# AdaLN modulation in a two-layer transformer kernel: shift and scale made as columns by one-column products

## Chip, core and metric

The kernel runs as one program on one core of a Trainium2 chip. The metric is the device time of a run in microseconds (us), from its first to its last instruction; the median of three runs is compared. Names of engines in the rows: PE is TensorE (matmul), PEld its weight loads, DVE is VectorE, ACT is ScalarE, POOL is GpSimd, SP is SyncE, which issues DMAs.

## What is computed

Two transformer layers over x (1024 rows of 512). Each has an attention branch and a feed-forward branch, and before each branch the rows are layernormed, scaled and shifted by vectors that come from a condition c (AdaLN); a third vector gates the branch's output. From the reference:

```python
mod = (_silu(L0_c) @ L0_wmod).reshape(L0_c.shape[0], 6, 1, -1)
sa, ca, ga, sb, cb, gb = (mod[:, 0], mod[:, 1], mod[:, 2], mod[:, 3], mod[:, 4], mod[:, 5])
ga = (2 * (ga >= 0) - 1) * jnp.maximum(jnp.abs(ga), 0.25)
gb = (2 * (gb >= 0) - 1) * jnp.maximum(jnp.abs(gb), 0.25)
h = _layernorm(x, axis=-1) * (1 + ca) + sa
x = x + ga * _L0_attn_ref(h, ...)
h = _layernorm(x, axis=-1) * (1 + cb) + sb
x = x + gb * _L0_ffn_ref(h, ...)
# the same again for layer 1, with L1_c, L1_wmod and its own attention and experts
```

Here c is 1 x 512 and wmod 512 x 3072, both f32, so each of the six vectors of a layer is a product of one row of 512 with a 512 x 512 matrix. The branches are a quantized attention, a low-rank-adapted feed-forward, a second attention, and a mixture of experts with low-rank adapters.

## The kernel before

The program is a row of phases; each is a block in which every engine has its own instruction stream, and no engine enters a block before all have left the last. Within a block, semaphores order the engines. The edit touches the four layernorm phases (`layernorm_phase`, run 0 to 3, called here first, second, third and fourth stage: 0 to 44 us, 979 to 1015.5, 1236.6 to 1263.5 and 1728.8 to 1752.6) and the output phase of the second attention (`layer1_output_phase`, 1681 to 1700 us).

`Modulation` holds the 512 x 512 f32 parts of wmod as SBUF tiles, 128 partitions by 4 blocks k by 512 (`mod0a_w`, `mod0b_w`, `mod1a_w`, `mod1b_w`). `silu_c` holds silu(c) as columns, 128 partitions by layer and k. `make_silu_rows` (L146) has VectorE copy each column broadcast to a 128 x 128 tile `silu_rows` (four tiles), with which as stationary operand a matmul yields the same row of 512 on all 128 partitions. Such a row is what a gate needs (`make_row` L181, `take_gate` L186), since a gate multiplies along the free axis.

Scale and shift are needed per partition instead, since the layernormed rows are first transposed (L313, so that a feature is a partition) and ScalarE applies them as its per-partition `scale` and `bias` (L335, L338). `make_columns` (L159) therefore makes the two rows in PSUM banks 4 and 5, by 8 matmuls of 512 moving columns, each f32 in two passes, and `take_columns` (L166) reads the diagonal: VectorE multiplies each 128 x 128 block of the row with the identity and sums it (L173, eight times, four columns for shift and four for scale, into `column`), and adds one to the scale (L178). `column_made`, `diagonals` and `column_taken` are the semaphores of these steps, `rows_done` that of `silu_rows`.

A layernorm phase on each engine:

- VectorE: `silu_rows`, then for each half of the rows (four tiles of 128 x 512) statistics (L254, L257), variance plus epsilon (L261), ScalarE's square root awaited, a reciprocal (L265) with one Newton step, and the normalised tiles (L276). In the second half it takes the columns: behind the normalised tiles in stages one to three, before the reciprocal in the fourth (`gate_first`). In the fourth stage it next takes the gate (L192 to L197). Then come eight pieces of `hT`, high and low parts for the split products of the next phase: ScalarE writes the high part of even pieces, VectorE casts that of odd ones (L286) and subtracts all low parts (L288), at last the gate in stage two.
- TensorE: first of all the columns' product, then (fourth stage only) the gate's row, then eight pieces of four transposes each (L313), at last the gate's row in the first and second stage. The third stage has no gate; that of its layer is made in the output phase, after two pieces.
- ScalarE: loads of weights in some stages, the two square roots (L326), then, when `column_taken` says so, the affine steps L335 and L338 in the order of the pieces, with four buffers.
- GpSimd works in the second stage on the weights of the feed-forward (L1084 among others). SyncE issues the loads of wmod.

In the output phase TensorE transposes `attended` (L1894) piece by piece, ScalarE copies each out (L1920), VectorE subtracts; VectorE makes `silu_rows` ahead of that.

## Time and profile before

| | us |
|---|---|
| Median of the three runs | 1811.9 |
| Lowest and highest of them | 1811.73, 1813.33 |
| The profiled execution | 1815.9 |
| Span in its trace | 1814.0 |
| TensorE busy | 1675.2 (92%) |
| TensorE's weight loads | 1344.5 (74%) |
| VectorE busy | 1192.8 (66%) |
| ScalarE busy | 1008.7 (56%) |
| GpSimd busy | 724.9 (40%) |

All times of rows are us from the start of the span. The profiled execution is one execution of the program, 4.0 us above the median of the timed ones; shares of busy time are averages over all phases, so that a stage of 30 us has to be read by its own rows.

### The profile page before, as it was taken

Reading aid. Unit: us, or ns where it says so; the run is one execution under the profiler, and the core shown is the slowest. Engines: PE = TensorE matmul, PEld = TensorE weight load, DVE = VectorE, ACT = ScalarE, POOL = GpSimd, SP = SyncE. Lnnn points to the kernel's source line nnn. Section 1 sums busy time; section 2 is a strip of 40 time slices with the busy share of each in tenths; the row PEclk is TensorE's granted clock in tenths of the full one; section 3 lists DMA queues with packets and bytes.
Section 4 is the critical chain, followed back from the end, with each engine's and each line's share of the span. In section 5 each row is a group of like instructions: output and inputs, shape, how many; then the busy total and the mean of one; then the engine's idle time right before and its main releaser. Section 6 shows DMA issues by size and latency. Waiting matters only on the chain. (4 is left out here: it accounts for less than half of the span.)

```text
span 1814.0 us, 28444 instructions
## 1 busy us (share of the span) xinstructions
PE 1675.2 (92%) x10115; PEld 1344.5 (74%) x10115; DVE 1192.8 (66%) x2924; ACT 1008.7 (56%) x2229; POOL 724.9 (40%) x656
## 2 busy tenths in 40 slices
PE   4899999999999999999997799996779999999778
PEld 2698999999999999899885588784645555554557
DVE  5667777677677777777667533355876777773475
ACT  2477777777877777777773211102216666666131
POOL 3286675756747567485531200000532222211200
PEclk8999999999999999999999899997959999999889
DMA  7101000000010100100003112005000000000021
GB/s 187 37 13 30 19 24 26 23 30 18 25 36 13 30 19 24 30 13 24 18 7 88 67 53 65 2 1 184 1 1 1 1 1 1 1 1 1 30 45 47
DMA packets 72358, 56.07 MB, mean 31 GB/s; under 512 B 23023, under 2 KB 54447, under 8 KB 72219
## 3 DMA queue, kind: packets, MB, share of 16 engines
q1 hardware_dynamic: 70634, 53.47, 10.2%
q8 instruction: 83, 1.36, 0.3%
q10 hardware_dynamic: 1584, 0.79, 0.2%
q14 instruction: 57, 0.46, 0.1%
HBM read 52.14 MB, written 2.10 MB: 30 GB/s over the span
## 5 line engine op out<-in xcount | busy, mean ns | idle before, releaser
L746 PEld LDWEIGHTS psum<-a_probsT,a_v 128*128 128x128 f32 x2304 | 294.7, 191 | 25.6 <-issue 3.9
L746 PE MATMUL psum<-a_probsT,a_v 128*128 128x128 f32 x2304 | 299.2, 275 | 1.7 <-ACT a_probsT L956 1.6
L845 DVE CUSTOM_DVE_ANT_0 psum<-psum,a_keys_allowed 128x128 f32<-128x128 f32 (+7 forms) x256 | 195.7, 764 | 83.0 <-PE psum L77 74.4
L939 ACT ACTIVATE a_probs<-psum,a_neg_max 128x128 f32<-128x128 f32 (+7 forms) x256 | 190.7, 745 | 66.6 <-DVE a_neg_max L845 58.2
L1827 ACT ACTIVATE a_probsT<-psum 128x512 f32<-128x512 f32 (+3 forms) x384 | 174.6, 497 | 86.4 <-PE psum L1664 62.4
L948 ACT ACTIVATE a_probs<-a_probs,a_row_inv 128x128 f32<-128x128 f32 (+7 forms) x256 | 201.1, 786 | 27.9 <-DVE a_row_inv L852 27.7
L609 POOL TENSOR_TENSOR a_turned_pool<-a_q_sum,a_sine 64x512 f32<-64x512 f32 x62 | 79.3, 1278 | 287.8 <-DVE a_q_sum L831 286.6
L875 DVE TENSOR_TENSOR a_ctxT_lo<-psum,a_ctxT_hi 128x128 fp32r<-128x128 f32 x256 | 73.7, 288 | 172.7 <-ACT a_ctxT_hi L962 172.6
L956 ACT COPY a_probsT<-psum 128x512 f32<-128x512 f32 (+3 forms) x384 | 173.2, 488 | 18.7 <-PE psum L734 16.6
L865 DVE SCALAR_TENSOR_TENSOR a_sumT<-psum,a_scale_o,a_sumT 128x512 f32<-128x512 f32 x248 | 173.6, 742 | 0.9 <-PE psum L760 0.7
L734 PE MATMUL psum<-ident,a_probs 128*128 128x128 f32 x1152 | 168.9, 274 | 0.7 <-ACT a_vT L933 0.5
L1759 DVE CUSTOM_DVE_ANT_0 psum<-psum,a_allowed 128x128 f32<-128x128 f32 (+3 forms) x256 | 123.6, 501 | 57.8 <-PE psum L1678 57.3
L75 PE MATMUL psum<-a_kT_hi,a_qT_lo 128*128 128x512 f32 (+3 forms) x384 | 151.1, 393 | 0.8 <-DVE a_kT_lo L618 0.8
L1661 PE MATMUL psum<-hT_hi,hT_lo 128*128 128x512 f32 (+3 forms) x384 | 145.5, 404 | 1.0 <-ACT a_probsT L1827 0.8
L1678 PE MATMUL psum<-hT_lo,hT_hi 128*128 128x512 f32 (+3 forms) x384 | 143.1, 414 | 2.4 <-issue 0.8
L831 DVE SCALAR_TENSOR_TENSOR a_q_sum<-psum,a_scale_q,a_q_sum 128x512 f32<-128x512 f32 x186 | 138.7, 747 | 4.4 <-PE psum L688 2.5
L734 PEld LDWEIGHTS psum<-ident,a_probs 128*128 128x128 f32 x1152 | 134.4, 142 | 2.8 <-issue 1.2
L77 PE MATMUL psum<-a_kT_hi,a_qT_hi 128*128 128x512 f32 (+3 forms) x384 | 133.3, 347 | 0.0
L76 PE MATMUL psum<-a_kT_lo,a_qT_hi 128*128 128x512 f32 (+3 forms) x384 | 132.9, 346 | 0.0
L1362 POOL TENSOR_TENSOR p_part<-p_qkv,p_rope 128x320 f32<-128x320 f32 x16 | 18.2, 1157 | 270.3 <-DVE p_qkv L1442 270.3
L962 ACT CAST a_ctxT_hi<-psum 128x128 fp32r<-128x128 f32 x256 | 67.3, 263 | 101.8 <-PE psum L746 99.9
L1661 PEld LDWEIGHTS psum<-hT_hi,hT_lo 128*128 128x128 f32 x384 | 74.6, 196 | 53.0 <-ACT a_probsT L1827 44.4
(348 smaller groups left out, 3963.7 us busy)
## 6 DMA issues: line engine op xcount, KB each, us to landing
a_raw_o<-in_L_attn_qw_o SPq DMA_DIRECT2D x32, 256.0 KB, 2.8
a_raw_q<-in_L_attn_qw_q SPq DMA_DIRECT2D x31, 256.0 KB, 3.3
mod1b_w<-in_L_wmod SPq DMA_DIRECT2D x4, 1024.0 KB, 11.3
mod0a_w<-in_L_wmod SPq DMA_DIRECT2D x3, 1024.0 KB, 13.0
mod0b_w<-in_L_wmod SPq DMA_DIRECT2D x3, 1024.0 KB, 7.0
f_raw<-in_L_ffn_down_w SPq DMA_DIRECT2D x10, 256.0 KB, 3.1
f_raw<-in_L_ffn_gate_w SPq DMA_DIRECT2D x10, 256.0 KB, 3.3
f_raw<-in_L_ffn_up_w SPq DMA_DIRECT2D x10, 256.0 KB, 3.6
```

The lines of the kernel that those rows point to most:

```text
L75: pe.matmul(out, lhs_lo, rhs_hi, start=start, stop=False)
L734: last = nc.tensor.transpose(bank(use)[:, tile(j - c * TPH)], probs[:, u % 3, tile(j)], mem.ident[:, :])
L746: last = nc.tensor.matmul(bank(use)[:, 0:P], v[:, g % 2, j, :], probsT[:, u % 2, j, :], start=(j == 0), stop=(j == i))
L831: nc.vector.scalar_tensor_tensor(out=total, in0=bank(("part", key, k))[:, :], scalar=scale_of(key, k), in1=total, op0=ALU.mult, op1=ALU.ad ...
L845: nc.vector.tensor_tensor_reduce(out=scores, in0=scores, in1=keys_allowed[:, S - (i + 1) * P:S], scale=-1.0, scalar=-MASKED, op0=ALU.add, ...
L865: nc.vector.scalar_tensor_tensor(out=total, in0=bank(use)[:, :], scalar=scale_o[:, j, h:h + 1], in1=total, op0=ALU.mult, op1=ALU.add).then ...
L939: nc.scalar.activation(probs[:, u % 3, 0:(i + 1) * P], score[u % 2][:, 0:(i + 1) * P], ACT.Exp, bias=neg_max[:, h % 2, i:i + 1], scale=-1. ...
L948: nc.scalar.activation(row, row, ACT.Copy, scale=row_inv[:, h % 2, i:i + 1]).then_inc(weighed.sem, 1)
L956: nc.scalar.copy(probsT[:, u % 2, c * TPH:c * TPH + keys, :].rearrange("p j q -> p (j q)"), bank(use)[:, 0:keys * P]).then_inc(turned_out. ...
L1661: last = nc.tensor.matmul(out[:, first:HALF], kB[:, h % 2, tile(j)], qB[:, h // 2, b * HALF + first:(b + 1) * HALF], start=True, stop=not ...
L1678: nc.tensor.matmul(y_bank[n % SLOTS][:, 0:keys], qA[:, h // 2, tile(i)], kA[:, h % 2, c * HALF:c * HALF + keys], start=True, stop=True).th ...
L1827: nc.scalar.activation(probsT[:, s % SLOTS, h, first:HALF], x_bank[n % SLOTS][:, first:HALF], ACT.Exp).then_inc(exped.sem, 1)
```

## The change

Only the edit, lines that only move or pass arguments left out:

```diff
-    def make_silu_rows(self, dve, silu_rows):
+    def make_silu_rows(self, act, silu_rows):
         for k in range(KT):
-            self.nc.vector.tensor_copy(silu_rows[:, k, :], self.mem.silu_c[:, self.layer, k:k + 1].broadcast_to([P, P])
-                                       ).then_inc(self.mem.modulation["rows_done"], 1)
+            self.nc.scalar.copy(silu_rows[:, k, :], self.mem.silu_c[:, self.layer, k:k + 1].broadcast_to([P, P])
+                                ).then_inc(self.mem.modulation["rows_done"], 1)
...
-    def make_columns(self, pe, pair, silu_rows, rows_used):
+    def make_columns(self, pe, pair):
-        pe.wait_ge(self.mem.modulation["rows_done"], KT * rows_used)
         for c, n in enumerate(pair):
-            last = self.multiply(pe, n, silu_rows, self.mem.bank[4 + c])
+            pe.wait_ge(self.mem.modulation[f"w_in{n}"], 16 * (self.layer + 1))
+            for piece in range(KT):
+                for k in range(KT):
+                    last = self.nc.tensor.matmul(self.mem.bank[4 + c][:, piece:piece + 1],
+                                                 self.w[:, self.parts.index(n), k, piece * P:(piece + 1) * P],
+                                                 self.mem.silu_c[:, self.layer, k:k + 1], start=(k == 0), stop=(k == KT - 1))
         last.then_inc(self.mem.modulation["column_made"], 1)
-    def take_columns(self, dve, pair, diagonals):
+    def take_columns(self, dve, pair):
         at = 4 * self.layer + (0 if pair[0] == 0 else 2)
-        number = self.number(pair[0])
-        dve.wait_ge(self.mem.modulation["column_made"], number)
-        for c in range(2):
-            for k in range(KT):
-                self.nc.vector.scalar_tensor_tensor(
-                    out=diagonals[c][:, k * P:(k + 1) * P], in0=self.mem.bank[4 + c][:, k * P:(k + 1) * P], scalar=1.0,
-                    in1=self.mem.ident[:, :], op0=ALU.mult, op1=ALU.mult,
-                    accum_out=self.mem.column[:, at + c, k:k + 1]).then_inc(self.mem.modulation["diagonals"], 1)
-        dve.wait_ge(self.mem.modulation["diagonals"], 2 * KT * number)
-        self.nc.vector.tensor_scalar(self.mem.column[:, at + 1, :], self.mem.column[:, at + 1, :], 1.0, None, ALU.add
+        dve.wait_ge(self.mem.modulation["column_made"], self.number(pair[0]))
+        self.nc.vector.tensor_copy(self.mem.column[:, at, :], self.mem.bank[4][:, 0:KT])
+        self.nc.vector.tensor_scalar(self.mem.column[:, at + 1, :], self.mem.bank[5][:, 0:KT], 1.0, None, ALU.add
                                      ).then_inc(self.mem.modulation["column_taken"], 1)
...
         @block.vector
         def _(dve):
-            modulation.make_silu_rows(dve, silu_rows)
...
         @block.tensor
         def _(pe):
-            modulation.make_columns(pe, pair, silu_rows, rows_used)
+            modulation.make_columns(pe, pair)
...
         @block.scalar
         def _(act):
             if first_weight and "loads" in first_weight:
                 first_weight["loads"](act)
+            if has_gate:
+                modulation.make_silu_rows(act, silu_rows)
             for half in range(NHALF):
...
         @block.scalar
         def _(act):
+            late.make_silu_rows(act, silu_rows)
             for i, (half, k) in enumerate(pieces):
                 act.wait_ge(a_turned, i + 1)
...
         @block.vector
         def _(dve):
-            late.make_silu_rows(dve, silu_rows)
```

The operands of the columns' product change places: a 128 x 128 block of wmod is stationary and one column of `silu_c` moves, so that the product comes out as a column. The product for a gate (`make_row`) stays as it is. The third stage makes no `silu_rows` any more; the others and the output phase have them from ScalarE, and the counts that `make_row` awaits follow. Lines of the changed kernel are two to four lower than before: L324 for L326, L333 and L336 for L335 and L338, L309 for L313, L261 for L265, L189 for L192; L165 is the columns' matmul, L174 and L175 are their copy and addition.

TensorE at the fourth stage: the columns' product (8 of the 12 rows of 512 columns), the gate's row (the other 4), the transposes; before:

```order
L77 MATMUL psum<-o_wT_hi,hT_hi 128x512
L1857 UNCONDITIONAL_BRANCH
L302 UNCONDITIONAL_BRANCH
L155 MATMUL psum<-mod1b_w,ln_silu_rows 128x512 x12
L313 MATMUL psum<-ident,ln_normed 128x128 x32
```

and in the changed kernel:

```order
L77 MATMUL psum<-o_wT_hi,hT_hi 128x512
L1855 UNCONDITIONAL_BRANCH
L298 UNCONDITIONAL_BRANCH
L165 MATMUL psum<-silu_c,mod1b_w 128x1 x32
L155 MATMUL psum<-mod1b_w,ln_silu_rows 128x512 x4
L309 MATMUL psum<-ident,ln_normed 128x128 x32
```

The eight wide products became 32 with one moving column, at the same place; the gate's row stands behind them as before.

VectorE in the second half of the fourth stage, where the columns are taken before the reciprocal; before:

```order
L261 TENSOR_SCALAR ln_y<-ln_mean_var 128x4
L173 SCALAR_TENSOR_TENSOR ln_sign,column<-psum,ident 128x128 x4
L173 SCALAR_TENSOR_TENSOR ln_size,column<-psum,ident 128x128 x4
L178 TENSOR_SCALAR column<-column 128x4
L265 RECIPROCAL ln_root<-ln_std 128x4
```

and in the changed kernel:

```order
L257 TENSOR_SCALAR ln_y<-ln_mean_var 128x4
L174 COPY column<-psum 128x4
L175 TENSOR_SCALAR column<-psum 128x4
L261 RECIPROCAL ln_root<-ln_std 128x4
L263 TENSOR_TENSOR ln_newton<-ln_root 128x4
```

Nine steps became two, and they stand where the nine stood.

ScalarE at the second stage; before:

```order
L962 CAST a_ctxT_hi<-psum 128x128
L441 UNCONDITIONAL_BRANCH
L319 UNCONDITIONAL_BRANCH
L326 ACT_TABLE_LOAD
L326 ACTIVATE ln_std<-ln_y 128x4 x2
L335 ACTIVATE ln_h<-psum,column 128x512
```

and in the changed kernel:

```order
L439 UNCONDITIONAL_BRANCH
L315 UNCONDITIONAL_BRANCH
L149 COPY ln_silu_rows<-silu_c 128x128 x4
L324 ACT_TABLE_LOAD
L324 ACTIVATE ln_std<-ln_y 128x4 x2
L333 ACTIVATE ln_h<-psum,column 128x512
```

The four copies of `silu_rows` came from VectorE and stand ahead of the table load and the roots.

## Rows read from the trace of the kernel before

**Rows 1.** The page's first line.

```profile
span 1814.0 us, 28444 instructions
```

**Rows 2.** Timeline, third stage: start us, us, engine, line, operation, out<-in, count [idle before].

```profile
1241.97 10.10 PE L155 MATMUL psum<-mod1a_w,ln_silu_rows 128*128 128x512 f32 x16 [6.34 <-DMA mod1a_w<-in_L_wmod]
...
1254.13 0.78 ACT L335 ACTIVATE ln_h<-psum,column 128x512 f32<-128x512 f32 x1 [7.65 <-DVE column L178]
```

**Rows 3.** Timeline, second stage.

```profile
979.23 2.62 DVE L149 COPY ln_silu_rows<-silu_c 128x128 f32<-128x128 f32 x4 [0.32 <-PEq L441]
...
984.49 9.14 PE L155 MATMUL psum<-mod0b_w,ln_silu_rows 128*128 128x512 f32 x16 [6.80 <-DMA mod0b_w<-in_L_wmod]
...
996.06 0.78 ACT L335 ACTIVATE ln_h<-psum,column 128x512 f32<-128x512 f32 x1 [5.06 <-DVE column L178]
...
1001.39 5.72 PE L155 MATMUL psum<-mod0b_w,ln_silu_rows 128*128 128x512 f32 x8
...
1005.85 3.14 POOL L1084 TENSOR_TENSOR f_down_a<-f_raw_down_a,f_down_a 16x1376 fp32r<-16x1376 f32 x1
...
1006.09 4.05 DVE L288 TENSOR_TENSOR hT_lo<-ln_h,hT_hi 128x512 fp32r<-128x512 f32 x2
...
1010.07 0.42 DVE L286 CAST hT_hi<-ln_h 128x512 fp32r<-128x512 f32 x1
...
1010.52 1.29 DVE L288 TENSOR_TENSOR hT_lo<-ln_h,hT_hi 128x512 fp32r<-128x512 f32 x2
```

**Rows 4.** Timeline, fourth stage.

```profile
1728.86 0.63 DVE L149 COPY ln_silu_rows<-silu_c 128x128 f32<-128x128 f32 x4 [0.32 <-PEq L1857]
...
1729.55 10.57 PE L155 MATMUL psum<-mod1b_w,ln_silu_rows 128*128 128x512 f32 x24 [1.73 <-DVE ln_silu_rows L149]
...
1740.20 0.17 DVE L265 RECIPROCAL ln_root<-ln_std 128x4 f32<-128x4 f32 x1
...
1743.04 0.68 DVE L192 TENSOR_SCALAR ln_sign<-psum 128x512 f32<-128x512 f32 x1
...
1745.80 0.69 DVE L288 TENSOR_TENSOR hT_lo<-ln_h,hT_hi 128x512 fp32r<-128x512 f32 x1
```

**Rows 5.** Timeline, first stage.

```profile
14.18 9.60 PE L155 MATMUL psum<-mod0a_w,ln_silu_rows 128*128 128x512 f32 x16 [14.18 <-DMA mod0a_w<-in_L_wmod]
...
31.09 0.63 ACT L547 ACTIVATE a_first_w<-a_raw_v 128x512 f32<-128x512 int32 x1 [2.84 <-DMA a_first_scale<-in_L_attn_scales_v]
```

**Rows 6.** Timeline at three places, and groups by line (ns min/median/max, first and last start).

```profile
1020.67 0.98 PEld L1166 LDWEIGHTS psum<-f_low_bT,f_low_a 80*128 80x128 f32 x4
...
1030.09 0.53 PEld L1166 LDWEIGHTS psum<-f_low_bT,f_low_a 80*128 80x128 f32 x4
...
106.04 1.95 PE L746 MATMUL psum<-a_probsT,a_v 128*128 128x128 f32 x16
...
L1166 PEld LDWEIGHTS psum<-f_low_bT,f_low_a x88: 189/192/337, 1020.7 to 1157.3; 80*128 80x128 f32 x88
L746 PE MATMUL psum<-a_probsT,a_v x2304: 270/275/415, 77.0 to 969.7; 128*128 128x128 f32 x192
```

**Rows 7.** Windows: us, busy PE (x), PEld, DVE, ACT, POOL, PEclk, DMA share, GB/s.

```profile
1242.00:1248.00 6.00, 6.00 (x7) 2.46 (x8) 5.52 (x20) 0.21 (x1) 0.00 (x0) 0.50 1.05 388
1330.00:1336.00 6.00, 5.26 (x22) 3.94 (x21) 5.78 (x21) 0.94 (x3) 1.75 (x3) 0.50 0.00 0
```

**Rows 8.** Timeline, output phase.

```profile
1681.61 1.94 PE L1894 MATMUL psum<-ident,attended 128*128 128x128 f32 x8 [1.08 <-PEq L1502]
...
1682.73 0.58 ACT L1920 CAST hT_hi<-psum 128x512 fp32r<-128x512 f32 x1 [2.97 <-PE psum L1894]
```

**Rows 9.** Windows, stretches without a matmul ahead of a fall of the clock.

```profile
1235.70:1237.70 2.00, 0.00 (x0) 0.00 (x0) 1.68 (x6) 1.05 (x1) 0.00 (x0) 1.00 0.04 1
1007.30:1012.40 5.10, 0.00 (x0) 0.00 (x0) 5.03 (x7) 0.78 (x1) 1.69 (x1) 1.00 0.00 0
```

**Rows 10.** Group by line, ScalarE copies of 128x128.

```profile
L962 ACT CAST a_ctxT_hi<-psum x256: 253/265/287, 77.5 to 970.1; 128x128 fp32r<-128x128 f32 x128
```

More of the change, by code:

```diff
@@ L129, in counters @@
     def counters(nc, mem):
-        names = [f"w_in{n}" for n in range(6)] + ["column_made", "diagonals", "column_taken", "rows_done", "row_made", "gate_step", "gate_done"]
+        names = [f"w_in{n}" for n in range(6)] + ["column_made", "column_taken", "rows_done", "row_made", "gate_step", "gate_done"]
         return {name: mem.semaphores.enter_context(nc.semaphore("mod_" + name)) for name in names}
@@ L238, in layernorm_phase @@
         sign, size = sb("sign", [P, D]), sb("size", [P, D])
-        rows_used = run + 1 + (run == 3)
+        rows_used = run + 1
         (stats_done, moments, y_done, root_done, rstd_done, normed_done,
@@ L262, in _ @@
                 if half and gate_first:
-                    modulation.take_columns(dve, pair, (sign, size))
+                    modulation.take_columns(dve, pair)
                 dve.wait_ge(*root_done.after(run, half + 1))
@@ L278, in _ @@
                 if half and not gate_first:
-                    modulation.take_columns(dve, pair, (sign, size))
+                    modulation.take_columns(dve, pair)
             if gate_first:
@@ L1889, in _ @@
                 if i == 2:
-                    late.make_row(pe, 2, silu_rows, 4)
+                    late.make_row(pe, 2, silu_rows, 3)
                 if i >= 2:
```

## The prediction, made before the changed kernel was run

> **What bounds the kernel now.** The program is a chain of phases with a common start, and most of its 1814.0 us [rows 1] are TensorE work that the edit does not touch. So I read the timeline of the stages with the edited lines one by one, four layernorm stages and the output phase, and asked of each which wait ends last before ScalarE's first affine step (L335). From that step on, ScalarE and VectorE run the stage to its end, and the next phase starts with its end.
>
> In the third stage [rows 2] TensorE starts when the load has landed, works 10.10 us on two 512-column rows, VectorE picks the diagonals, and ScalarE, idle for 7.65 us, starts at 1254.13. Nothing else is late, and what follows goes in step with ScalarE. In the second [rows 3] it is the same with 9.14 us from 984.49 and ScalarE at 996.06 after 5.06 us, but there VectorE and GpSimd then block each other: two subtractions take 4.05 us until GpSimd's 3.14 us instruction from 1005.85 is over, and the same two take 1.29 from 1010.52. In the fourth [rows 4] TensorE waits 1.73 us for VectorE's condition rows, then runs columns and gate row in one piece of 10.57 us at the high clock; ScalarE starts there without the columns being last, and VectorE is the engine without gaps: diagonals, then the reciprocal at 1740.20, the gate at 1743.04, the first low part at 1745.80. In the first [rows 5] TensorE's two rows start at 14.18, but ScalarE is held until 31.09 by a load of scales.
>
> **The product: how many passes, and how long is one.** Per pair of columns, 8 instructions of 512 moving columns become 32 of one moving column, each with its own 128x128 weights. The trace shows each f32 product as two passes, with a weight load each (x16 for 8 instructions [rows 2]); so 64 loads with nearly nothing to stream. No row shows a one-column product. Nearest are products with little behind each load of 128 columns: at the low clock four loads take 0.98 us from first start to last end, the last of them 0.337, so (0.98 - 0.337) / 3 = 0.214 us from one to the next; at the high clock 0.53 and 0.19, so 0.113 [rows 6]. L746, f32 in two passes as here, does 16 in 1.95 us with 0.275 for one, (1.95 - 0.275) / 15 = 0.112 [rows 6]. A pair therefore takes 64 x 0.214 = 13.7 us at the low clock and 64 x 0.113 = 7.2 at the high one. The old 16 passes took 16 x 0.857 = 13.7 at the low level (7 in 6.00 us [rows 7]) and half of that at the high one. The count of weights replaces the count of columns and saves TensorE nothing; everything hangs on the clock.
>
> The Trainium skill (TensorE: Matmul & The Clock Gate, Part 3, "The mechanism") says that a weight load overlaps matmuls in flight only when its row group differs, which speaks against this change: here all groups are the same, and every load would wait. The trace disagrees, since L746's matmuls last 0.275 us each and still come every 0.112 us, loads included.
>
> **The clock.** From 1242 to 1248 TensorE streamed 512-column passes without a gap at 0.50 [rows 7], and then the clock rose: all 16 passes took 10.10 us [rows 2], not 13.7. From 1330 to 1336 it was busy for 5.26 of 6.00 us, with weight loads for 3.94 and mostly 128-column matmuls, and the clock stayed at 0.50 [rows 7]. Loads and short matmuls so filled the engine's time without raising the clock. The one-column passes are the extreme of that, so I take it that they neither raise the clock nor hold it up. The skill (same page, Part 1) says only that the gate looks at how busy the engine has been and that activity releases it; by that, busy loads could count, which is the first rival below. The row from 1330 does not speak for it.
>
> **Stage by stage, at the low clock.**
> - Third: 1241.97 + 13.7 = 1255.7. Taking the columns costs VectorE two steps of the reciprocal's size, 2 x 0.17 [rows 4], beside the transposes. At the low clock the first four transposes reach ScalarE 1.12 us after their start (1681.61 to 1682.73 [rows 8]): 1256.8 against 1254.13, **+2.7 us**. The eight diagonals that go, some 1.8 us between the end of the rows at 1252.07 and the columns' release of ScalarE at 1254.13, are already in this difference. ScalarE sets the pace behind, the stage ends 2.7 later.
> - Second: 984.49 + 13.7 + 1.1 = 999.3 against 996.06, +3.2. VectorE is 2.62 us earlier [rows 3] and merely waits longer. Of the lateness some is absorbed, since until 1009.0 VectorE gets only one step in per GpSimd instruction. Counting the steps so, three more are left after GpSimd's end, a cast of 0.42 and two subtractions of 0.65: 1.7 us later than now. Bounds: 0.5 (GpSimd is done sooner, having been less disturbed) and 3.2 (all of it). I take the count, **+1.8**. The gate row behind it took 5.72 us from 1001.39 and was wanted only behind the last low part, 1010.52 + 1.29 = 1011.8, 4.7 after its end; starting some 3 us later it is still in time.
> - Fourth: the weights are in long since and no rows are waited for, so TensorE starts near 1728.86. Dense work ended at 1729.55 - 1.73 = 1727.8. The clock was still up 2.0 us after the last matmul in one place and 5.1 in another [rows 9]; I take 4.2, the middle shifted to the longer one because here only 1 us passes before passes come again: until 1732.0 go 28 passes, the other 36 take 7.7, to 1739.7. The gate row next, eight passes from the low clock, took 5.72 us in [rows 3]: 1745.4. VectorE, 2.3 us earlier by the rows' 0.63 and the diagonals' 1.7, has long been ready and waits. Its four steps take 1745.80 - 1743.04 = 2.76: first low part at 1748.2 for 1745.80, **+2.5** with 0.1 for ScalarE's late start. Bounds: +1.5 and +5.
> - First: 14.18 + 13.7 + 1.1 = 29.0, before 31.09, and the columns too are there: **0**; the cover is 2.1 us thick.
> - ScalarE's rows: four copies of 128x128, the nearest at 0.265 [rows 10], 1.1 us, in the first, second and fourth stage ahead of a root that it waits for longer than that; in the output phase between 1681.6 and its first operand at 1682.73 [rows 8], just covered: **0**, up to 0.4 each if not. VectorE loses the rows there at no gain.
>
> Sum: 0 + 1.8 + 2.7 + 0 + 2.5 = +7.0 us. The profiled execution took 1815.9 us (span 1814.0), so 1822.9 in its own terms; it lies 4.0 above the median of the three timed runs, 1811.9, and against that the forecast is **1818.9**.
>
> **The rivals.**
> - *Loads count as work; the clock rises as before* (faster). In the second stage 9.14 us is about 5 passes at 0.857 and 11 at half of it, so the clock was low for 4.3 us: 20 + 44 passes, 9.3 us, ScalarE at 994.4, -1.7, of which about 1.2 reach the end; third (low for 6.0) 28 + 36 passes, 10.1 us, ScalarE at 1252.8, -1.3; fourth 7.2 + 3.4 us of row, ended by 1739.5, VectorE sets the stage and is 2.2 earlier. Sum -4.7: 1807.2. It decides from the pass at which the rise comes: in the third stage 0.214 n + 0.113 (64 - n) must stay below 1254.13 - 0.6 - 1241.97 = 11.6, n below 43. For it: nothing in the trace isolates loads. Against: 1330 to 1336.
> - *It is partly absorbed* (no change): the fourth stage keeps the high clock through its columns (+0), GpSimd ends sooner (+0.5), third +1.5 because the clock rises in the transposes: +2.0, 1813.9.
> - *Each load waits for the matmul before it*, the skill's rule: by rows at least 0.337 + 0.19 at the low clock, 64 x 0.5 = 32 us per pair. First stage 14.2 + 32 + 1.1 = 47.3 for 31.1, +16, the others +18 each: some +70, 1882. L746 speaks against it, but streams 128 columns, not one.
>
> **How the numbers follow.** Forecast 0.67, loads count 0.15, absorbed 0.14, serial loads 0.04. The forecast's own range is +3.7 to +12, 1815.6 to 1824. For 8 in 10 the range reaches down to the first rival's time, since that is the least tested assumption, and up to the late ends of the second and fourth stage: 1807 to 1825. What can be told from no change here is 0.2%, 3.6 us: faster 0.15, same 0.14, slower 0.71.
>
> **What would show it.** In the profile after: one-column loads 0.21 us apart and PEclk 0.50 in the second and third stage until the transposes or the gate row; ScalarE's L335 (L333 then) at about +3 in both; in the fourth the clock falling some 3 us into the columns and the reciprocal, then the gate, waiting for TensorE; the first stage's third weight step still the last before L333. Wrong if the clock rises during the columns (then first rival), if loads come further apart than 0.22, or if ScalarE's copies stand before a waiting TensorE in the output phase.

## The result, and the profile after

Timed against the kernel before in the same session, the changed kernel took 1825.1 us in the median of five executions (1821.9 to 1828.5) where the kernel before took 1811.9 (1810.7 to 1813.3): ratio 1.0073, interval 1.0053 to 1.0092, so 9.6 to 16.7 us slower. The forecast was 1818.9, range 1807 to 1825; the sign was right, the size was not. Ratios and medians leave out one execution that ran at a mean clock of 0.74 and took 2117.9 us (in the kernel with the fourth stage alone changed).

The timeline of the changed kernel at the places of [rows 2 to 5] (start us, us, engine, line, operation, out<-in, count, idle before):

```profile
14.48 13.81 PE L165 MATMUL psum<-silu_c,mod0a_w 128*128 128x1 f32 x64 [14.48 <-DMA mod0a_w<-in_L_wmod]
...
30.58 0.63 ACT L545 ACTIVATE a_first_w<-a_raw_v 128x512 f32<-128x512 int32 x1 [2.86 <-DMA a_first_scale<-in_L_attn_scales_v]
...
984.81 13.81 PE L165 MATMUL psum<-silu_c,mod0b_w 128*128 128x1 f32 x64 [6.75 <-DMA mod0b_w<-in_L_wmod]
...
999.67 0.78 ACT L333 ACTIVATE ln_h<-psum,column 128x512 f32<-128x512 f32 x1 [9.78 <-PE psum L309]
...
1248.19 13.82 PE L165 MATMUL psum<-silu_c,mod1a_w 128*128 128x1 f32 x64 [6.69 <-DMA mod1a_w<-in_L_wmod]
...
1263.06 0.78 ACT L333 ACTIVATE ln_h<-psum,column 128x512 f32<-128x512 f32 x1 [11.26 <-PE psum L309]
...
1739.03 10.25 PE L165 MATMUL psum<-silu_c,mod1b_w 128*128 128x1 f32 x64 [1.05 <-PEq L1855]
...
1749.14 5.67 PE L155 MATMUL psum<-mod1b_w,ln_silu_rows 128*128 128x512 f32 x8
...
1754.85 0.69 DVE L189 TENSOR_SCALAR ln_sign<-psum 128x512 f32<-128x512 f32 x1 [2.47 <-PE psum L155]
...
1757.62 0.69 DVE L284 TENSOR_TENSOR hT_lo<-ln_h,hT_hi 128x512 fp32r<-128x512 f32 x1
```

Read it against the working: the pair of columns takes 13.8 us in three stages where 13.7 was forecast, ScalarE starts 14.9 us after TensorE in the second and in the third stage (14.8 forecast), the fourth stage has 10.25 and 5.67 us for columns and gate row, and VectorE there waits 2.47 us for the row that it never waited for before. In the first stage the scales' load still ends last.

The granted clock (PEclk, 1.00 for the high level and 0.50 for the low one) while these products run, with TensorE and its loads busy for the whole of each window (columns as in [rows 7]):

```profile
14.50:28.20 13.70, 13.70 (x65) 13.70 (x66) 5.04 (x18) 1.46 (x3) 1.14 (x1) 1.00 0.81 224
985.00:998.00 13.00, 13.00 (x62) 13.00 (x63) 7.37 (x22) 0.20 (x1) 2.33 (x5) 0.50 0.70 179
1249.00:1261.00 12.00, 12.00 (x57) 12.00 (x58) 5.27 (x18) 0.20 (x1) 0.00 (x0) 0.50 1.06 369
1739.03:1743.00 3.97, 3.97 (x36) 3.97 (x36) 3.56 (x13) 2.36 (x6) 0.00 (x0) 0.99 0.53 168
1744.00:1749.00 5.00, 5.00 (x25) 5.00 (x25) 4.01 (x12) 0.21 (x1) 0.00 (x0) 0.50 0.75 153
```

In the second and third stage passes with one moving column do not raise the clock in 13 us, and in the fourth they do not hold it up: it falls 3.9 us into them (3.1 and 1.9 us in the two later profiles). The first window doesn't fit: its PEclk reads 1.00, yet its passes come as far apart as those at 0.50. The trace's record of the clock begins only at 36.3 us, and ahead of it the profile prints 1.00; so for the first stage I go by the passes, and that the clock was low there is concluded and not read. The third stage's products, grouped by line (ns min/median/max, first and last start):

```profile
L165 PEld LDWEIGHTS psum<-silu_c,mod1a_w x64: 288/333/338, 1248.2 to 1261.6; 128*128 128x128 f32 x64
L165 PE MATMUL psum<-silu_c,mod1a_w x64: 352/352/374, 1248.2 to 1261.7; 128*128 128x1 f32 x64
```

A load lasts 0.333 us and a matmul 0.352, yet a pair of the two comes every 0.214 us: they overlap. With the pair at 13.8 us and not 32, the rival of serial loads is gone.

**Where the time went.** I cut each profile at the first event of each phase. The lengths in us, for the kernel before (two profiles) and the changed one (three); "again" and "third" are runs told below:

| Phase | before | before, again | changed | changed, again | changed, third |
|---|---|---|---|---|---|
| second stage | 36.9 | 36.9 | 38.3 | 38.6 | 37.8 |
| third stage | 27.1 | 26.9 | 30.2 | 30.5 | 30.5 |
| fourth stage | 24.0 | 24.0 | 26.0 | 27.6 | 27.6 |
| the three | 88.0 | 87.8 | 94.5 | 96.7 | 95.9 |
| feed-forward | 220.6 | 222.5 | 224.6 | 222.5 | 221.9 |
| second attention | 417.8 | 417.5 | 419.1 | 419.9 | 417.8 |
| all but the three | 1726.0 | 1726.5 | 1732.1 | 1727.8 | 1724.9 |
| span | 1814.0 | 1814.3 | 1826.6 | 1824.5 | 1820.8 |

The three stages lose 7.8 us in the mean (95.7 against 87.9), for a forecast of 7.0. Between the first profiles of the two kernels (12.6 us) another 6.1 us lie outside these three stages, 4.0 of them in the feed-forward, whose code did not change. Its start, windows of the kernel before and of the changed one:

```profile
1016.04:1026.04 10.00, 8.72 (x39) 7.42 (x40) 3.19 (x5) 2.12 (x4) 0.95 (x1) 0.67 0.17 50
```

```profile
1017.89:1027.89 10.00, 8.78 (x34) 7.54 (x35) 3.19 (x5) 2.12 (x4) 0.95 (x1) 0.50 0.14 41
```

And a place in its middle where TensorE waits for VectorE for 1.97 us, in the kernel before, in the changed one, and in the second profile of the changed one:

```profile
1171.00:1181.00 10.00, 8.03 (x34) 6.09 (x33) 2.17 (x5) 0.00 (x0) 0.00 (x0) 1.00 0.00 1
```

```profile
1176.00:1186.00 10.00, 8.03 (x29) 6.23 (x28) 2.17 (x5) 0.00 (x0) 0.00 (x0) 0.83 0.00 0
```

```profile
1172.50:1182.50 10.00, 8.03 (x35) 6.02 (x34) 2.17 (x5) 0.00 (x0) 0.00 (x0) 1.00 0.00 0
```

TensorE is busy for the same 8.03 us around the same gap, and in one and the same kernel the clock once falls for a third of the window and once stays up. What decides that, no row shows. The kernel before differs from itself too: its second profile was at the low clock for the first 11 us of the feed-forward, its first for 6.7 (222.5 us for 220.6). So part of the first pair's 12.6 us is such chance, and the experiments had to say how much.

### The profile page after: what moved, and what is told of

It reads as the page before. It is cut to its first block and busy times, and to the rows that moved or that the text cites. A ratio compares the mean times of both kernels' runs of the same rounds, so it can differ in the third digit from the quotient of the medians.

```text
span 1826.6 us, 28760 instructions
## 1 busy us (share of the span) xinstructions
PE 1701.0 (93%) x10307; PEld 1390.0 (76%) x10307; DVE 1179.8 (65%) x2844; ACT 1012.3 (55%) x2245; POOL 724.3 (40%) x656
## 6 DMA issues: line engine op xcount, KB each, us to landing
mod0a_w<-in_L_wmod SPq DMA_DIRECT2D x3, 1024.0 KB, 13.3
```

## The experiments

All ratios are to the kernel before, timed on the same chip in the same session (its medians were 1813.9, 1814.5, 1814.8 and 1812.5 us); "us" behind a ratio is the ratio's excess times that median.

### The changed kernel again, and the kernel before again

> The changed kernel once more, nothing edited. Theory A (the stages with the edit lose some 6 us, and the phases behind them lose as much again through low-clock stretches that fall differently from one execution to the next): the time lies again 10 to 16 us above the kernel before with a spread of several us between executions, the three late stages measure the same as in the first profile within 0.5 us, and the untouched phases (feed-forward 224.65 us in the first profile, 220.64 in the kernel before) differ from the first profile by 1 to 4 us. Theory B (the loss in the untouched phases is a fixed consequence of the change): feed-forward again 224 to 225 us.

> The kernel before once more, for a second profile. Theory A: its feed-forward phase also differs between two profiles, by one or more low-clock stretches (steps of about 1.7 us), so somewhere in 220 to 225 us. Theory B: 220.6 within 0.3 us as in its first profile.

Ratio 1.0066 (1.0049 to 1.0084), +12.0 us, with executions from 1820.7 to 1827.9. The profiles are in the table: stages within 0.3 us of the first in the second and third, 1.7 longer in the fourth where 0.5 was the most expected (the clock fell at 3.1 us, the columns took 11.00 us, and the gate row 6.58 instead of 5.67, most of it at the low clock), feed-forward 222.5 in both kernels. Theory B fails: the 4.0 us of the first pair are no fixed cost. The kernel with the third stage alone changed shows it once more: nothing ahead of its feed-forward is changed, and its feed-forward took 224.0 us. The loss of 12 us stayed all the same, and in this profile 2 us of it lie in the second attention (419.9).

### How many columns move: 256, then 128

The changed kernel with the moving operand read several times; only the first column of each product is kept.

```diff
-                    last = self.nc.tensor.matmul(self.mem.bank[4 + c][:, piece:piece + 1],
+                    last = self.nc.tensor.matmul(self.mem.bank[4 + c][:, piece:piece + 256],
                                                  self.w[:, self.parts.index(n), k, piece * P:(piece + 1) * P],
-                                                 self.mem.silu_c[:, self.layer, k:k + 1], start=(k == 0), stop=(k == KT - 1))
+                                                 self.mem.silu_c[:, self.layer, k:k + 1].broadcast_to([P, 256]), start=(k == 0), stop=(k == KT - 1))
```

> As the changed kernel, but each of the 64 passes moves 256 columns (the condition's column read 256 times), of which only the first is kept; the weights, their loads, their number and the reads by VectorE are the same. Theory A (what keeps the clock low is that one moving column is nearly no streaming): the passes still come 0.214 us apart at the low clock, but the clock rises in the second and third stage as it did with 512-column products, and stays high in the fourth; the pair takes about 9.3 and 10.1 us instead of 13.8, the fourth stage is 2 us shorter than before, and the whole is 2 to 6 us faster than the kernel before (ratio 0.997 to 0.999). Rival (weight loads of 128 columns, one for each 0.2 us, hold the clock down whatever moves, or a pass gets longer by its columns): the clock stays at 0.50 for 13.8 us or the pair gets longer than that; ratio 1.005 or more.

Ratio 1.0089 (1.0075 to 1.0104), +16.1 us: slower still. The rival had two halves; the first, that the loads hold the clock down, did not come, the second, that a pass gets longer by its columns, did, and theory A's time failed by it. Third stage, timeline and two windows:

```profile
1244.33 16.51 PE L165 MATMUL psum<-silu_c,mod1a_w 128*128 128x256 f32 x64 [6.95 <-DMA mod1a_w<-in_L_wmod]
...
1246.00:1249.00 3.00, 3.00 (x8) 2.37 (x8) 2.52 (x13) 0.21 (x1) 0.00 (x0) 0.50 1.05 386
1255.00:1258.00 3.00, 3.00 (x15) 2.62 (x14) 0.00 (x0) 0.00 (x0) 0.00 (x0) 1.00 1.05 388
```

The clock rises, with the same 64 weight loads. But the pair takes 16.51 us: 7 or 8 passes in 3 us at the low level and 14 at the high one are 0.43 and 0.21 us each: a 256-column f32 pass takes half of what a 512-column one takes (0.857 and 0.43), which was in [rows 7] to be read, and I had priced it at half of that. So the same with the number that does fit behind a load, 128:

> As the changed kernel, but each of the 64 passes moves 128 columns (the condition's column read 128 times), of which the first is kept. The run with 256 showed an f32 pass of 256 columns 0.213 us or more apart at the high clock, so 128 should fit behind a weight load at either level. Theory A (one moving column is no streaming and leaves the clock low; 128 stream without a gap, as the 512-column passes of the kernel before did): passes 0.214 us apart at the low clock and about 0.11 at the high one, the clock rises within the pair in the second and third stage, so pairs of 9 to 11 us, fourth stage about 2 us shorter than in the kernel before; whole 2 to 6 us faster than before, ratio 0.9965 to 0.999. Rival (loads at this rate hold the clock down): pairs of 13.8 us at 0.50 as with one column, ratio 1.006 to 1.008.

Ratio 0.9993 (0.9984 to 1.0002), -1.3 us, less than the 2 to 6 us of theory A. Third stage, the group of its products, and windows at its start, further on, and in the fourth stage:

```profile
1244.37 9.42 PE L165 MATMUL psum<-silu_c,mod1a_w 128*128 128x128 f32 x64 [7.11 <-DMA mod1a_w<-in_L_wmod]
...
L165 PE MATMUL psum<-silu_c,mod1a_w x64: 273/273/582, 1244.4 to 1253.5; 128*128 128x128 f32 x64
...
1244.37:1247.37 3.00, 3.00 (x14) 3.00 (x15) 2.92 (x10) 0.01 (x1) 0.00 (x0) 0.50 1.04 384
1250.00:1253.00 3.00, 3.00 (x29) 3.00 (x29) 0.52 (x2) 0.00 (x0) 0.00 (x0) 1.00 1.11 308
1730.30:1737.50 7.20, 7.20 (x64) 7.20 (x65) 6.72 (x20) 2.34 (x6) 0.00 (x0) 1.00 0.72 213
```

14 passes in 3 us at the low clock, as with one column, so 127 columns more cost nothing; and the clock rises, so the pair takes 9.42 us for 13.8, and in the fourth stage it stays up through all 64 passes, 7.2 us. The stages become 37.5, 25.7 and 22.0 us, 2.7 less than before. With passes, loads, operands and waits all equal, moving 128 columns instead of one is worth 13.3 us (from +12.0 to -1.3, uncertain by some 3.5). This settles what my clock paragraph rested on, and it gives the stage lengths that my first rival had for "the clock rises" in all but the second stage, where ScalarE started 1.0 us earlier and the end came 0.7 later; probably VectorE was then beside GpSimd's long instructions for longer, which no run separates.

### The rows on ScalarE alone

The kernel before with `make_silu_rows` on ScalarE in all five places.

> The kernel before with only the condition's rows moved from VectorE to ScalarE in all five places; columns as before. Theory A: second stage VectorE is 2.6 us earlier but the columns' product ends last, so at most 0.3 us; third 0; fourth TensorE starts some 0.3 us later than VectorE's rows allowed (ScalarE's copies take 0.89) while VectorE starts 0.66 earlier, about -0.3 to -0.6; in all 0 to -1 us, ratio 0.999 to 1.0005. Rival (the copies on ScalarE cost where they stand before a waiting TensorE): +0.5 us or more.

Ratio 1.0004 (0.9994 to 1.0015), +0.7 us: nothing that can be told from no change. In its fourth stage the copies stand before a TensorE that waits for them:

```profile
1725.89 0.89 ACT L149 COPY ln_silu_rows<-silu_c 128x128 f32<-128x128 f32 x4 [27.20 <-PEq L1857]
```

0.89 us for 0.63 on VectorE, and TensorE waited 1.97 us instead of 1.73 for them.

### Lateness alone

The kernel before, with 14 more VectorE steps ahead of the diagonals in the second to fourth stage.

```diff
...
         dve.wait_ge(self.mem.modulation["column_made"], number)
+        if self.number(pair[0]) > 1:
+            for i in range(14):
+                self.nc.vector.scalar_tensor_tensor(out=spare[:, i, :], in0=self.mem.bank[4][:, 0:P], scalar=1.0,
+                                                    in1=self.mem.ident[:, :], op0=ALU.mult, op1=ALU.mult)
...
```

> The kernel before with 14 more VectorE multiplications of 128x128 (about 0.2 us each, 2.9 us) ahead of the diagonals in the second, third and fourth stage, TensorE's work unchanged: only the lateness of the columns. Theory A (lateness costs its own time in the stage and no more; what the changed kernel loses behind the stages comes from TensorE having been at the low clock): stages +1.6, +2.9, +2.9, whole +7.4 us, ratio 1.004, the phases behind as in the kernel before. Rival (any shift of this size costs as much again in the phases behind): +11 to +15 us, ratio 1.006 to 1.008.

Ratio 1.0044 (1.0031 to 1.0058), +8.0 us, for stages of 37.8, 29.5 and 26.8 us, +6.2 together. The 14 steps took 2.86 us:

```profile
1252.14 2.86 DVE L173 SCALAR_TENSOR_TENSOR ln_spare<-psum,ident 128x128 f32<-128x128 f32 x14 [2.33 <-PE psum L155]
```

So 2.86 us of lateness made the stages 0.9, 2.6 and 2.8 us longer, and the whole 8.0 (5.6 to 10.5): about its own time, as theory A has it, and the rival's 11 to 15 is out.

### The change stage by stage

The kernel before with the changed columns in some stages only (rows on VectorE as before). The edit puts the changed body of `make_columns` and `take_columns` behind a condition on the stage:

```diff
+        if self.number(pair[0]) in (3,):
+            for c, n in enumerate(pair):
+                pe.wait_ge(self.mem.modulation[f"w_in{n}"], 16 * (self.layer + 1))
...
+            last.then_inc(self.mem.modulation["column_made"], 1)
+            return
         pe.wait_ge(self.mem.modulation["rows_done"], KT * rows_used)
```

> The kernel before, with the changed kernel's columns (one-column products, two VectorE steps) in the third stage alone. Theory A: third stage +3.3 us as measured in the changed kernel, and up to 2 us more in the second attention behind it, where the clock rises later: +3 to +5.5, ratio 1.0018 to 1.003. Rival (the loss behind the stages has nothing to do with them): +3.3.

> The kernel before, with the changed kernel's columns in the fourth stage alone, the gate's rows by VectorE ahead of them as before (the product no longer waits for them). Theory A: the clock falls some 4 us into the one-column products; stage +2 to +3.6 us and the experts' phase +0.5 to +1: +2.5 to +4.5, ratio 1.0014 to 1.0025. Rival (VectorE's saving of 1.7 us in diagonals makes up for it): 0 to +1.

> The kernel before, with the changed kernel's columns in the second stage alone. With the third alone (+5.0 us, of which the stage 2.9) and the fourth alone (+3.3 by the medians, +1.6 by the ratio) this completes the sum. Theory A (the parts add up, and the whole change costs 12.6 to 13.2): second alone +4 to +6 us, ratio 1.002 to 1.0035, of which the stage itself shows 1.5 and the rest lies in the feed-forward behind it. Rival (the parts do not add; the second stage costs only what it shows): +1 to +2, ratio 1.0005 to 1.001.

> The kernel before, with the changed kernel's columns in the first stage alone. Theory A (the cover by the scales' load holds, as forecast): the stage 43.4 to 44.2 us as in all profiles, ratio 0.999 to 1.001. Rival B (the missing 5 us come in behind the first stage, in the attention, whose length was 935.5 and 933.7 us in two profiles of the changed kernel and 934.6 twice in the kernel before): ratio 1.002 to 1.003.

> The kernel before, with the changed kernel's columns in the second and third stage. Parts add: +5.0, ratio 1.0027. Rival C: +8 to +10, ratio 1.0045 to 1.0055, with the second attention 2 us longer than in the kernel before (419 to 421 for 417.5).

> The kernel before, with the changed kernel's columns in the second, third and fourth stage; the condition's rows stay on VectorE. Parts add: +0.3 + 4.7 + 1.6 = +6.6, ratio 1.0036. Rival C (the three together cost more than their parts, through the phases behind them): +11 to +13, ratio 1.006 to 1.007.

> The changed kernel a third time. If the excess over the parts was a draw, ratio 1.004 to 1.0055; if it is fixed, 1.0065 to 1.0075 again.

| Changed in | ratio (interval) | us | seen in the changed late stages |
|---|---|---|---|
| rows only | 1.0004 (0.9994 to 1.0015) | +0.7 | -1.0 |
| first | 1.0011 (1.0001 to 1.0021) | +2.0 | 0 |
| second | 1.0002 (0.9991 to 1.0013) | +0.4 | +0.5 |
| third | 1.0026 (1.0017 to 1.0035) | +4.7 | +2.9 |
| fourth | 1.0009 (1.0000 to 1.0018) | +1.6 | +3.6 |
| second and third | 1.0035 (1.0023 to 1.0047) | +6.3 | +3.0 |
| second to fourth | 1.0062 (1.0048 to 1.0076) | +11.2 | +6.5 |
| all (the changed kernel) | 1.0073, 1.0066, 1.0077 | +13.2, +12.0, +14.0 | +6.6, +8.8, +8.0 |

The two clearest places, third stage of the one and fourth of the other:

```profile
1243.63 13.81 PE L166 MATMUL psum<-silu_c,mod1a_w 128*128 128x1 f32 x64 [6.41 <-DMA mod1a_w<-in_L_wmod]
...
1258.50 0.78 ACT L350 ACTIVATE ln_h<-psum,column 128x512 f32<-128x512 f32 x1 [10.43 <-PE psum L328]
```

```profile
1728.07 10.99 PE L166 MATMUL psum<-silu_c,mod1b_w 128*128 128x1 f32 x64 [1.05 <-PEq L1872]
...
1738.92 6.59 PE L155 MATMUL psum<-mod1b_w,ln_silu_rows 128*128 128x512 f32 x8
...
1745.54 0.69 DVE L207 TENSOR_SCALAR ln_sign<-psum 128x512 f32<-128x512 f32 x1 [3.39 <-PE psum L155]
```

Each part's time is uncertain by 1.6 to 2.0 us, so the five parts' sum, 9.4, is uncertain by some 4, and the whole's 12 to 14 lies inside that. The chance excess that the third run of the changed kernel was meant to expose isn't there: the whole is 12 to 14 three times. Second to fourth together are +11.2, and with rows and first (+2.7) that is 13.9. The fourth stage costs 3.6 us in its own profile and 4.9 as the difference of the two combined kernels, and the medians of the same executions are 3.3 apart, so the 1.6 by its ratio is probably low.

Against what was expected: the third alone came out as theory A has it, the fourth alone by its ratio below theory A, the second alone without the 4 us of theory A, the first alone between its two theories. Second to fourth lies where rival C had it, 4.5 us above the 6.7 of its parts, but that difference is itself uncertain by some 4 (by the medians 9.8 against 7.9), and second and third lies between the sum and rival C. That the parts cost more together is so neither shown nor excluded.

In the three of these kernels that have the third stage changed it took 29.9, 29.8 and 29.8 us, +2.8 to +2.9 for +2.7 forecast, and 30.2 to 30.5 in the changed kernel.

For the first stage the profile shows the cover as forecast, the scales' load last before the affine step:

```profile
14.10 13.81 PE L166 MATMUL psum<-silu_c,mod0a_w 128*128 128x1 f32 x64 [14.10 <-DMA mod0a_w<-in_L_wmod]
...
29.83 0.63 ACT L562 ACTIVATE a_first_w<-a_raw_v 128x512 f32<-128x512 int32 x1 [2.72 <-DMA a_first_scale<-in_L_attn_scales_v]
...
30.37 0.76 ACT L350 ACTIVATE ln_h<-psum,column 128x512 f32<-128x512 f32 x1
```

The stage took 43.5 us and the kernel's ratio still is 1.0011. Where these 2.0 us (0.2 to 3.8) lie, one profile can't tell; its span was 1812.9, less than either of the kernel before.

### TensorE kept busy to a stage's end

The changed kernel with products of no use behind TensorE's last work in a stage.

```diff
             if has_gate and not gate_first:
                 modulation.make_row(pe, gate, silu_rows, rows_used)
+            w = modulation.w[:, modulation.parts.index(pair[0]), :, :]
+            for i in range((0, 9, 3, 3)[run]):
+                nc.tensor.matmul(mem.bank[7][:, :], w[:, i % KT, 0:P], w[:, i % KT, :], start=True, stop=True)
```

> The changed kernel with 512-column f32 products of no use behind TensorE's last work in the second (9 products), third and fourth stage (3 each), into a PSUM bank that nobody reads, while TensorE would wait for the stage's end. Theory A (the phases behind the stages lose because TensorE enters them at the low clock): the feed-forward starts at the high clock or reaches it earlier than the 11 us of the changed kernel, -3 to -5 us there; third and fourth -0 to -2 each, since the added products run at the low clock themselves and may end up to 1 us late; whole 4 to 8 us faster than the changed kernel, ratio to the kernel before 1.002 to 1.005. Rival (the clock at a phase's start does not matter, or the products cost what they give): ratio 1.006 to 1.008 as the changed kernel.

Ratio 1.0045 (1.0031 to 1.0059), +8.2 us, 4 to 6 less than the changed kernel. The first 5 us of the feed-forward and 10 us around the start of the second attention, in this kernel and then in the changed one:

```profile
1017.00:1022.00 5.00, 3.54 (x18) 3.10 (x18) 0.86 (x2) 0.95 (x2) 0.95 (x1) 0.69 0.02 5
1265.00:1275.00 10.00, 6.60 (x36) 4.39 (x35) 6.59 (x11) 5.93 (x9) 0.00 (x0) 1.00 0.01 2
```

```profile
1018.00:1023.00 5.00, 3.88 (x17) 3.23 (x18) 0.76 (x2) 0.95 (x2) 0.85 (x1) 0.50 0.02 5
1268.00:1278.00 10.00, 4.69 (x21) 4.19 (x22) 5.86 (x9) 5.11 (x8) 0.00 (x0) 0.69 0.01 2
```

The second attention (from 1269.34 here, from 1272.70 there) starts at 1.00 instead of running at 0.50 for its first 9 us, and is 415.4 us long for 417.8 to 419.9. The feed-forward starts high, falls after 1.7 us and is up again after 5.1.

### Versions meant to be faster

Columns as before in the first and second stage, with 128 moving columns in the third and fourth, rows on ScalarE; then the same with the filling products (9, 4 and 4).

> Columns as before in the first and second stage; in the third and fourth the stationary weights with 128 moving columns of the run before last; rows on ScalarE as in the change. From the stages measured there (third 25.7 for 27.0 us, fourth 22.0 for 24.0, second as before): theory A expects -3.4 us against the kernel before, ratio 0.9975 to 0.999. Rival (chance in the phases behind decides): 0.999 to 1.001.

> The same with products of no use at the ends of the second (9), third (4) and fourth stage (4), where the clock is still high when they start. Theory A: the three phases behind start at the high clock or reach it several us earlier: the feed-forward -2 to -4 us, the second attention -2 to -4, the experts -2 to -3, so -10 to -14 us against the kernel before, ratio 0.992 to 0.995. Rival (the clock falls at the phases' starts anyway, since their first matmuls are sparse): -3.4, ratio 0.998.

Ratio 0.9989 (0.9980 to 0.9998), -2.0 us, with stages of 36.3, 24.4 and 22.0 us; and 0.9965 (0.9951 to 0.9979), -6.4 us, faster than both kernels. Theory A holds for the first, and for the second its 10 to 14 us did not come: the filling is worth 4.4 us (uncertain by 3), about half of what I expected of it. From the profile of the filled one, the products of the third stage and the start of the second attention; then the first block of the second attention, without and with the filling:

```profile
1255.67 3.60 PE L334 MATMUL psum<-mod1a_w 128*128 128x512 f32 x8
...
1260.59:1268.59 8.00, 6.77 (x44) 5.64 (x45) 3.64 (x4) 3.10 (x4) 0.00 (x0) 1.00 0.00 2
```

```profile
1262.70:1315.22 52.52, 40.55 (x216) 34.97 (x216) 43.36 (x52) 12.05 (x28) 26.22 (x24) 0.86 0.00 1
```

```profile
1260.59:1310.44 49.85, 37.32 (x216) 31.93 (x216) 43.16 (x52) 11.96 (x28) 26.21 (x24) 0.92 0.00 1
```

It had no low stretch at the start, and that block (the projections of the second attention) took 49.9 us for 52.5: the 8 us at the low clock had cost 2.7. The filled version of the changed kernel shows the same, 49.9 us for 52.4 to 53.1. And yet the whole second attention took 416.6 us, only 0.4 less than without: the block behind, with the same code, took 366.8 us for 364.5, with 57 us at the low clock for 51. That block lay between 364.1 and 367.9 us over all profiles, so this loss is of the size of chance and can't be put down to the filling.

## Why the prediction was right and wrong

- **Price of a pass, right.** 64 passes at 0.214 us were forecast from weight loads with other products behind them; 13.81 us were measured in the first three stages.
- **The clock, right.** One-column passes leave it low and let it fall, as [rows 7] made likely; the kernel with 128 moving columns shows it with nothing else changed. My first rival fails on that, not on its arithmetic: with the clock up, third and fourth stage came out 1.3 and 2.0 us shorter, for 1.3 and 2.2 worked out.
- **Serial loads did not come, as I held.** The Trainium skill (TensorE: Matmul & The Clock Gate, Part 3, "The mechanism") has a load overlap matmuls in flight only when its row group differs. All groups here are equal, and the changed kernel's rows show 0.333 and 0.352 us long steps every 0.214, so the trace disagrees with that sentence. The prediction left out that the same section also lets a load go ahead into a background weight buffer; the rows fit that, though they don't show where a load goes.
- **Second stage +1.8.** Measured +1.4, +1.7 and +0.9, and +0.5 alone. The absorption by GpSimd's instructions is as counted, and a little more of it.
- **Third stage +2.7.** Measured +3.2, +3.5, +3.5 (against 27.0), and +2.8 to +2.9 in the three kernels with the rows on VectorE. ScalarE followed TensorE by 14.87 us as worked out (14.8), and the end followed ScalarE by 9.64 as before. What is left is the load's landing, 5.7 and 6.0 us from the stage's start for 5.3 and 5.4 before, which I had held fixed; why it lands later I can't say. It isn't the one-column products, since in those three kernels it landed at 5.25 to 5.40.
- **Fourth stage +2.5.** Measured +1.9, +3.6, +3.6. The moment of the clock's fall was the unknown: forecast after 28 passes; the 64 passes took 10.25, 11.00 and 12.09 us, with some 36, 29 and 18 of them before it. The gate row was as priced from [rows 3] or a little shorter (5.67 and 5.45 for 5.72), or 0.9 longer, when the clock rose only near its end. The bounds of +1.5 and +5 held all three, and the 4.2 us that I took for the clock's fall was a choice between two rows: that its 28 passes lie in the middle of the three is partly luck.
- **ScalarE's rows and the first stage, 0.** No stage shows them, +0.7 and +2.0 us by the ratios; for the first stage that is just outside chance (by the medians +1.2), and I have not found it.
- **The step that failed** is the last line of the sum. It added the stages, and took the phases between them as fixed. So it put everything outside the three late stages at nothing. The stages were 7.8 for 7.0; the kernel was 12 to 14, so 4 to 6 us lay in the term that was put at nothing. The kernel before, whose three executions shown lay within 1.6 us, ranged from 1808.7 to 1819.6 over the sessions, and its feed-forward alone from 220.6 to 222.5 us, with low-clock stretches that are there in one execution and not in another. The bounds that I gave for the second and fourth stage allow at most 3.2 + 2.7 + 5 = 10.9 us, 1822.8; the range ended at 1825, and no line says what the 2.2 us between are for. The result lay 0.1 us above.

What stays open: of the 4 to 6 us beyond the stages, the experiments show that the block behind the third stage loses some 3 us when it is entered at the low clock (52.4 to 53.1 us for 49.9), but the kernel before enters it so too (52.5 and 52.3), and the filling took 4.4 us off the best version as well, so it isn't what sets the changed kernel apart. Against the mean of the two profiles before, the three have +5.9, +1.6 and -1.3 us outside the stages, a mean of 2.1. Only the experts' phase is clearly longer in all three (61.6, 62.1 and 61.5 us for 61.1 twice), by 0.6 in the mean.

The other 2 to 4 us are accounted for by which executions were profiled. The two of the kernel before took 1815.9 and 1816.2 us, 4.0 and 2.3 above the medians of their sessions; the three of the changed kernel lay 3.4 above, 0.1 below and 1.9 below theirs. So the spans are 9.8 us apart in the mean where the medians are 12 to 13, and the 2.7 us by which the two sides differ there make up the gap. In which phase a median execution of the kernel before is shorter than the two profiled ones, no profile shows. The best version speaks for the same: its three stages are 5.2 us shorter than in the profiles before, and its time is only 2.0 less. My forecast took 4.0 us off for the profiled execution, but used that execution's phases as if they were typical.

## What to carry to other kernels

Exchanging operands so that a product with one row becomes products with one column saved no TensorE time here, where each block of 128x128 f32 weights must be loaded for it (64 passes of 0.214 us for 16 of 0.857), and the clock no longer rose or stayed up. With 128 moving columns instead of one, if the result's bank has the room, the passes came as fast and the clock rose. When a change makes the clock differ in a stage, price the stage and then add to the range what the phases behind it can do, from several profiles of the unchanged kernel and not from one. Look also at where the profiled execution lies among the timed ones: a phase table from executions above the median hides that much of a loss. Filling a stage in which TensorE waits at the end took 4 to 6 us off one kernel and 4.4 off another, but check the next phases one by one, since a gain at the start of one can be hidden by the spread of another.

## What the runs showed of the hardware that I had not expected

- f32 passes of one and of 128 moving columns come equally far apart, 0.214 us at the low clock and 0.113 at the high one; 256 columns take 0.43 and 0.21.
- With the weights loaded at the same pace, 13 us of one-column passes, TensorE busy throughout, stayed at 0.50; in 128-column passes it was 0.50 for the first 3 us and 1.00 from 5.6 us on.
- The same gap of 1.97 us with 8.03 us of work around it lowered the clock in one execution of the changed kernel and not in another.
- Eight us at the low clock at the start of the second attention cost 2.7 us (52.5 us for 49.9).
- PEclk can print 1.00 at the start of a profile, ahead of the clock's first entry (36.3 us here), over passes that come 0.214 us apart, the pace of 0.50 elsewhere.
- Four copies of 128x128 from a broadcast column took 0.89 us on ScalarE for 0.63 on VectorE.
